# Attention with a mixture-of-experts layer on one core: tile rows are turned through DRAM and VectorE instead of on TensorE

## Time and profile before

| | |
|---|---|
| median of 3 runs | 583.53 us (583.46 to 583.60) |
| the profiled execution | 579.44 us, of it 577.6 us in the span of the trace |
| ACT busy | 500.6 us, 487.6 of them in 512 exponentials |
| PE busy | 537.2 us |
| DVE, POOL busy | 295.2 and 245.2 us |
| mean busy share of the 16 DMA engines | about 0.4 |
| the chain that ended last | PE 74%, ACT 11%, DVE 8% |

### The profile page before, as it was taken

The page is one execution under the profiler, slowest core; times in us unless marked ns, Lnnn a source line. Parts: engine busy times, 40 slices in busy tenths (PEclk is TensorE's granted clock), DMA queues, the critical chain, the costliest instruction groups (busy, mean ns, idle before and its releaser), DMA issues.

```text
span 577.6 us, 12513 instructions
## 1 busy us (share of the span) xinstructions
PE 537.2 (93%) x4620; PEld 244.5 (42%) x4620; DVE 295.2 (51%) x986; ACT 500.6 (87%) x552; POOL 245.2 (42%) x308
## 2 busy tenths in 40 slices
PE   8899988899899999999899999999989999999875
PEld 6323322234445555335344555433434554555212
DVE  4975698854334444544443344455333444344394
ACT  2699998899998888998888988889889889888993
POOL 4289910798244444456222344365412443432100
PEclk9999999999999999999999999999999999999998
DMA  7045311533244454233533355531434454562451
GB/s 261 25 120 146 117 48 27 188 101 119 75 123 167 147 193 156 84 101 129 160 124 106 112 190 170 168 101 52 145 95 138 152 167 128 174 190 73 163 226 61
DMA packets 44656, 75.47 MB, mean 131 GB/s; under 512 B 7584, under 2 KB 17872, under 8 KB 44080
## 3 DMA queue, kind: packets, MB, share of 16 engines
q1 hardware_dynamic: 39232, 63.71, 34.2%
q0 software_dynamic: 4544, 9.32, 5.3%
q10 hardware_dynamic: 816, 1.61, 0.7%
HBM read 33.88 MB, written 8.85 MB: 74 GB/s over the span
## 4 chain that ended last, share of the span: by engine, by line
PE 74%; ACT 11%; DVE 8%; issue 3%; DMA 2%; ACTq 1%; POOL 0%; POOLq 0%; DVEq 0%; SPq 0%
PE acc L732 32%; PE sc L697 12%; ACT ring L963 11%; PE aside_bank L776 10%; PE sc L793 10%; PE sc L765 3%; PE aside_bank L802 2%; DVE x L1352 1%; PE aside_bank L608 1%; DMA wr<-L_attn_W_k 1%; DMA xn<-token_out 1%; PE aside_bank L793 1%; PE aside_bank L592 1%; DVE blocks L1131 1%; DMA token_out<-work,token 1%
## 5 line engine op out<-in xcount | busy, mean ns | idle before, releaser
L963 ACT ACTIVATE ring<-sc 128x1024 f32<-128x1024 f32 x512 | 487.6, 1031 | 53.8 <-PE sc L697 53.1
L732 PE MATMUL acc<-ring,v 128*9 128x512 f32 x2048 | 249.2, 594 | 14.1 <-ACT ring L963 9.3
L544 POOL DMA_INDIRECT work<-normed,token x71 | 69.6, 981 | 201.5 <-DVE work L1322 176.2
L697 PE MATMUL sc<-qs,ks 32*128 32x512 f16 x1024 | 101.4, 384 | 8.8 <-ACT ring L963 6.5
L697 PEld LDWEIGHTS sc<-qs,ks 32*128 32x128 f16 x1024 | 26.3, 90 | 165.0 <-ACT ring L963 145.7
L732 PEld LDWEIGHTS acc<-ring,v 128*9 128x9 f32 x2048 | 40.7, 89 | 114.2 <-issue 80.5
L556 POOL DMA_INDIRECT token_out<-work,token x71 | 70.4, 992 | 38.9 <-issue 19.2
L1328 DVE TENSOR_SCALAR work<-aside_bank,xn 128x128 f32<-128x128 f32 x216 | 60.8, 344 | 24.2 <-PE aside_bank L776 24.2
L1339 DVE TENSOR_TENSOR work<-sc,xn 128x128 f32<-128x128 f32 x50 | 14.6, 292 | 108.6 <-PE sc L793 108.6
L776 PE MATMUL aside_bank<-work,xn 128*128 128x128 f32 x432 | 57.6, 276 | 0.0
L776 PEld LDWEIGHTS aside_bank<-work,xn 128*128 128x128 f32 x432 | 52.6, 192 | 1.1 <-issue 1.1
(11 more groups left out here) (202 smaller groups left out, 440.9 us busy)
## 6 DMA issues: line engine op xcount, KB each, us to landing
xn<-w_rest SPq DMA_DIRECT2D x54, 323.0 KB, 3.3
xn<-L_ffn_W SPq DMA_DIRECT2D x54, 256.0 KB, 2.8
w_last<-w_rest SPq DMA_DIRECT2D x17, 323.0 KB
w_last<-L_ffn_W SPq DMA_DIRECT2D x17, 256.0 KB
qs<-hl SPq DMA_DIRECT2D x60, 64.0 KB
ks<-hl SPq DMA_DIRECT2D x60, 64.0 KB
x<-L_attn_x SPq DMA_DIRECT2D x4, 512.0 KB, 8.7
w_rest<-L_ffn_W SPq DMA_DIRECT2D x8, 256.0 KB, 3.9
```

The source lines that it names most:

```text
L544: pool.indirect_dma_start(out=xt[t % TILE_BUFFERS], out_offset=None, in_=xh_d[:, :], in_offset=bass.IndirectOffsetOnAxis(ap=token[:, 0, t: ...
L697: last = nc.tensor.matmul(dst, ks[r:r + 32, kb * P:(kb + 1) * P], qs[r:r + 32, at], start=True, stop=not slow)
L732: last = nc.tensor.matmul(acc[32 * j:32 * j + VW, :], v9[:, b, kb, 4 * g + j, :], ring[:, (2 * n + j // 2) % UNITS, j % 2, :], start=(kb = ...
L963: nc.scalar.activation(ring[:, (2 * n + u) % UNITS, :, :], sc[HOME[2 * n + u]][:, :].rearrange("p (h c) -> p h c", h=2), ACT.Exp, scale=SC ...
```

## The change

- PE turns only tile 0. The other 70 tiles go another way: SP writes the gathered rows to DRAM as four stacks of 32 columns (`spread_rows`, 64 KB in runs of 128 bytes), reads them back so that each partition gets 512 contiguous bytes (`load_rows`, into `xq`, 2 buffers), and DVE turns blocks of 32x32 (`nc.vector.transpose` into `xr`) and scales and shifts them into `xsT` with a strided read (`columns`).
- In a full pair layer one (`aside_bank`) now stands ahead of the second layer (spare home, at column 0). DVE's order is columns of the next tile, relu, addition of b2.
- The wait for the spare home moves: the scores of m+3 wait for `tile_taken`, no longer those of m+2, and the general wait of other work is gone. `score_homes` deals the scores of m+2 past the spare home of m.
- POOL's gather waits for the write to DRAM (`rows_out`) instead of for DVE; DVE now counts one `tile_taken` per tile.
- Tables: 76 free pairs instead of 77; 31 light pairs instead of 33 from step 46 to 240, full ones 66 instead of 64; `SECOND_PAIRS` are 78, 90, 142, 206; two projections of batch 1 move (38, 44, 48, 50 instead of 38, 40, 46, 50), the ranks go from step 24 to 23; squares stand at a step whose pair is full.

```diff
@@ tables
-ROUTE_AT, RANKS_AT, SLOTS_AT, OWNER_AT, GATES_AT = 21, 24, 24, 37, 43
+ROUTE_AT, RANKS_AT, SLOTS_AT, OWNER_AT, GATES_AT = 21, 23, 24, 37, 43
-PLAIN_AT = {n: (1, r) for r, n in enumerate((38, 40, 46, 50))}
+PLAIN_AT = {n: (1, r) for r, n in enumerate((38, 44, 48, 50))}
...
-SQUARE_AT = {n + 5: piece for n, piece in PLAIN_AT.items() if piece[0] > 1}
-SQUARE_AT.update({n: (1, r) for r, n in enumerate((43, 45, 50, 54))})
+SQUARE_AT = {next(m for m in (n + 7, n + 5, n + 9) if m - 1 in BOTH): piece for n, piece in PLAIN_AT.items() if piece[0] > 1}
+SQUARE_AT.update({n: (1, r) for r, n in enumerate((43, 47, 53, 55))})
...
+ROWS_AT = {n: k + 3 for n, k in ONE_AT.items() if k + 3 < SLOT_TILES}
@@ score_homes
+        before = n - 2 if n - 2 in BOTH else None
         for u in range(2):
-            pair = order[0]
+            pair = next(k for k in order if before is None or k != spare[before])
@@ SP
+            def spread_rows(t):
+                k = t % TILE_BUFFERS
+                sp.wait_ge(xt_in[k], 16 * (t // TILE_BUFFERS + 1))
+                if t - TILE_BUFFERS >= 1:
+                    rows_are_home(sp, t - TILE_BUFFERS)
+                sp.dma_start(rows_d[k].rearrange("(j p) d -> p j d", j=4),
+                             xt[k].rearrange("p (j d) -> p j d", j=4)).then_inc(rows_out[k], 16)
+
+            def load_rows(t):
+                k = t % TILE_BUFFERS
+                rows_are_spread(sp, t)
+                wait(sp, columns_ok, t - 2)
+                sp.dma_start(xq[t % 2][:, :], rows_d[k].rearrange("(p i) d -> p (i d)", i=4)).then_inc(rows_home[t % 2], 16)
...
+                    if n in ROWS_AT:
+                        spread_rows(ROWS_AT[n])
+                        load_rows(ROWS_AT[n] - 1)
                     if n in WEIGHTS_AT:
                         weights(WEIGHTS_AT[n])
@@ PE
-                if n in TWO_AT:
-                    layer_two_and_turn(TWO_AT[n], n)
                 if n in ONE_AT:
                     layer_one(ONE_AT[n])
+                if n in TWO_AT:
+                    layer_two(TWO_AT[n], n)
...
-                        if n - 1 in BOTH:
-                            pe.wait_ge(tile_taken, TWO_AT[n - 1] + 1)
+                        if n - 2 in BOTH:
+                            pe.wait_ge(tile_taken, TWO_AT[n - 2])
@@ DVE
+                rows_are_home(v, t)
+                wait(v, columns_ok, t - 1)
+                nc.vector.transpose(xr[:, :], xq[t % 2][:, :]).then_inc(blocks_ok, 1)
+                v.wait_ge(blocks_ok, t)
+                nc.vector.tensor_scalar(xsT[t % 2].rearrange("p (t i) -> p i t", i=4),
+                                        xr[:, :].rearrange("p (i t) -> p i t", i=4), scale, offset, ALU.mult, ALU.add
+                                        ).then_inc(columns_ok, 1)
...
-                if n in TWO_AT:
-                    rows_and_columns(TWO_AT[n], n)
+                if ONE_AT.get(n, SLOT_TILES) + 1 < SLOT_TILES:
+                    columns(ONE_AT[n] + 1)
                 if n in ONE_AT:
                     relu(ONE_AT[n])
+                if n in TWO_AT:
+                    tile_out(TWO_AT[n], n)
```

109 lines of the change are left out of this document (57 added, 52 removed).

## The result

The changed kernel takes **590.46 us** (median of 4 runs, 589.08 to 591.93), beside 583.5 us of the kernel before: a ratio of 1.0112, 95% interval 1.0070 to 1.0155. The forecast was 580.3 us, faster; it is slower.

What follows compares the result with a forecast made beforehand. PE was taken to set full pairs' pace and ACT light pairs'; after the change ACT's exponentials bind full pairs. Terms -5.4 (steps 46 to 240), -1.3 (front), +3.5 (stacks) sum to -3.2: 583.5 to 580.3 us, range 576 to 588.

Steps and rivals of the forecast that it cites:

- The full pair: Full pair after the change: 4.58 us, before 4.53, since PE waits 0.31 us for ACT's two exponentials.
- PE at 4.27: Rival that ACT's new wait does not bind: full pairs at PE's 4.27 us, 560 us in all; chance 0.03.
- Squares cost nothing in a full pair: ACT in a full pair: a square fits between exponentials, 1.44 us against the 1.50 that pass anyway.
- From 46 to 240 without the stacks: 66 full pairs at 4.58 and 31 light at 3.67: 416.1 us against 421.5, -5.4, bounds -5.4 and -3.6.
- The stacks: Rows land late behind stack loads at steps 81, 145, 209, 225: 0.9 us each, +3.5, between 0 and 14.
- The front: Up to step 46's scores: moved projection against DVE's wait for tile 1's rows; scores near 115.4, -1.3 us.
- Rival 2: The rows' round trip becomes the bound in every full pair: 600 us, milder cases 586 to 589; chance 0.14, slower.
- X = 7.0 us: Landing time of the rows after `tile_out` from which the round trip decides a full pair; forecast landing 5 us.
- Rival 1: The rows come in time even behind a stack, so the four waits go: 576.8 us; chance 0.25.
- The other rule: Turn left on PE in the new order: PE's half 2.37 us, under ACT's 2.42; no stack waits, 576.8 us.

Runs made afterwards that it cites:

- first profile: Profiled execution of the changed kernel, 590.93 us, beside its first measurement of 590.46 us, 1.0112 of the kernel before.
- e7: e1 with the square of step 47 at step 51 and the squares of batches 2 and 3 back at their old steps: 576.66 us, 0.9936.
- e11: The kernel before with only the squares of batches 2 and 3 moved into full pairs: 576.99 us, 0.9946.
- e1: Changed kernel with the turn back on PE, no DRAM round trip or block turn: 575.40 us, 0.9850; repeated 572.95 us, 0.9898.
- e12: Changed kernel with rows ahead of the stack's loads, the stack in two halves, gates at step 41: 575.00 us, 0.9911.
- second profile: Profile of the same changed kernel, unchanged, when run again in sitting 4: 582.74 us, 1.0031 of the kernel before.
- sitting 4: Runs taken together on one chip: kernel before 579.70 us, changed kernel again 582.74, e1 572.95, e4 572.97, e5 572.70.
- e4: e1 plus the rows' DRAM round trip in 128-byte descriptors, which nobody uses: 581.04 us, 0.9967; repeated 572.97 us, 0.9865.
- e5: e4 with the idle rows written whole, 128 descriptors of 512 bytes: 573.98 us, 0.9885; repeated 572.70 us, 0.9865.

## Why the prediction was wrong, point by point

Two terms of the sum failed. The four pairs behind stacks were put at 3.5 us and cost 4.7 and 6.5 in the two profiles. What stands behind DVE's wait at the front was put at nothing, and cost 3.6 and 1.4. The largest piece of the first profile, 9.5 us of late exponentials, was in no term, and its cause stays open.

**The full pair: right.** 4.58 us, PE at 4.27 excluded by ACT's two exponentials, no extra behind a light pair. PE's own half was mis-sized (2.31, not 2.11), which changed nothing, since ACT's 2.42 stood over it. With the turn it is 2.42 and not 2.37, level with ACT's. "Squares cost nothing in a full pair" was right for ACT's pace (e7, e11).

**From 46 to 240 without the stacks: nearly right.** Forecast 416.1; e1 and e12, which have no late waits, 417.6. The 1.5 us between lie inside the bound that I gave (-5.4 to -3.6). A slip stands in the sum behind it: the pieces of the kernel before add up to 419.1 and not 419.7, so its small waits are 2.4 us and the bound should have been -3.0.

**The stacks: the mechanism and the four places were right, the term was mis-sized.** I forecast 0.9 us each, 3.5; measured were 4.7 in the first profile and 6.5 in the second. The steps of the sum, for the third of them in the first profile (timelines of DVE and SP):

```profile
476.52 0.28 DVE L1373 TENSOR_TENSOR work<-sc,w_last 128x128 f32<-128x128 f32 x1
...
486.86 0.31 DVE L1355 STREAM_TRANSPOSE xr<-xq 128x128 f32<-128x128 f32 x1 [5.47 <-issue]
```

```profile
478.06 2.50 SPq L361 DMA_DIRECT2D qs<-hl  x4
480.60 2.51 SPq L361 DMA_DIRECT2D ks<-hl  x4
...
483.84 0.51 SPq L418 DMA_DIRECT2D xq<-tile_rows  x1
```

`tile_out` ends at 476.80, the load is issued at 483.84, 7.0 us later (forecast 6.75), and DVE has the rows at 486.86, 3.0 us after the issue. I had taken 1.9, the landing of a transfer of 32 KB by itself. But this one has 64 KB, and is issued 0.6 us behind the write of the next tile, another 64 KB in 512 descriptors, on the same queue. By my own sum a landing at 8.7 leaves a wait of 0.1 us, so one at 10.1 leaves 1.5; measured are 1.2 at this place. At the other three places the issue was late as well: four DMAs of the stack took 3.16, 3.32 and 3.06 us of SP and not 2.5, the load was issued 7.7, 7.8 and 7.6 us after `tile_out`, and DVE had the rows 2.6, 2.3 and 2.4 later, 10.0 to 10.3 in all. That is the slow stack of rows 9, in three places of four, where I had counted four cases in eleven. In the second profile the issue came 7.2 to 8.3 after `tile_out` and the rows 10.2 to 10.7. So both terms, 6.75 for the issue and 1.9 for the landing, were too small.

**The front: the wait was found, and what stands behind it was not.** I had the write landed at 110, the load at 112.5 and the relu over at 114.3; the second profile has 110.66, 112.64 and 114.46. The step that failed is the sentence that DVE's wait "stands ahead of the relu of tile 0", taken as the whole of it. It also stands ahead of the gates at step 43. From them it goes over POOL's additions to its split, and from the split to a square which I had priced at nothing because it fits beside PE. Whether it fits says nothing on whether its input is there. In the first profile that chain held ACT for 2.4 us, and pair 48 lost 2.0. The other cost is one that no sum of busy times has: PE's idle time ahead of these pairs was followed by a stretch at half the clock, 1.6 us at pair 50 in the first profile and 1.2 at pair 46 in the second, where the chain over POOL costs 0.1 alone. I counted -1.3 us up to the scores of step 46, and they came nearly as forecast (115.39 and 115.94, forecast 115.4). The loss came behind them, 3.6 us (first profile) and 1.4 (second).

**What no step had: late signals.** 9.5 us of the first profile, and none in the fourth sitting. My sum was made against an execution of 579.44 us, and I noted that the median stood 4.1 above it without asking why. That may have been the sign: the trace of that execution has 0.1 us of lateness, and the medians of the same kernel in the sittings without it are 579.7 to 581.2. That the runs around it had lost their 4 us in this way is argued, since none of them has a trace. In an undisturbed sitting the kernel before takes 579.7, and the changed kernel 582.7.

In the terms of the undisturbed execution the forecast was 576.2, measured were 582.9 (the second profiled execution): 3.0 from the stacks, 1.4 at the pairs 46 and 48, 1.5 from small waits, 0.5 ahead of step 46, 0.3 at the end.

**The rivals.** Rival 2 came closest: the round trip did decide, though not in every full pair. Its threshold of X = 7.0 us was not reached in plain pairs, where the rows landed between 4.4 and 7.0 us after `tile_out`, half of them within 5.5 (forecast 5). It was exceeded behind stacks alone, at 8 to 11. The rule of the Trainium skill ("DMA: Bandwidth & Descriptors", section "Specifications") that below 512 bytes a transfer misses the line rate holds for the packets: in e4's and e5's traces of sitting 4 one of 128 bytes takes 13 ns and one of 512 bytes 27 ns, so four small ones take twice as long for the same bytes. For a write of 64 KB that is 0.42 us of the 16 engines instead of 0.22, too little to bring this rival about, and with nobody waiting the kernels stood at 0.9865 both. Rival 1's 576.8 would have needed e12's edits. The other rule of the Trainium skill that I weighed ("VectorE: DVE Perf Modes", section "Rules for kernel authors"), to turn on TensorE, had a sum of its own in the prediction, 576.8 us with the median of then; e1 measured 575.4. That the two are so near is in part luck, since 4.1 us of late exponentials are in its profile. By that rule the turn stays, and the runs agree.

## What to carry to other kernels

When a wait is put into an engine's queue, list everything behind it in program order, not only the operation that it is for, and follow each item to the engines that wait for it; here a wait whose end was forecast to 0.2 us went over DVE and POOL to ACT, and over DVE's relu to PE. Where PE is idle by it, look at the granted clock of the next few microseconds: here it cost as much again. A small transfer is priced by what is issued ahead of it, both in the issuing engine's time and on the queue, not by its own landing time alone. And where a profiled execution is faster than the median of the same kernel, ask what the others may have lost, and a comparison of two kernels needs both in one sitting.
